# Norm rows and key operands of a feature map lifted in fewer, larger transfers

## What is computed

```python
def feature_map(x, orf):                      # x: 32 wide, orf: 128 x 32
    proj = x @ orf.T / d_k ** 0.25
    norm = jnp.sum(x * x, axis=-1, keepdims=True) / (2.0 * math.sqrt(d_k))
    return (jnp.exp(proj - norm) + EPS) / math.sqrt(m)
q = feature_map(split(x @ Wq.T + bq), orf)
k = feature_map(split(x @ Wk.T + bk), orf)
v = split(x @ Wv.T + bv)
kv, ksum = einsum('nlm,nld->nmd', k, v), sum(k, axis=1)
out = einsum('nlm,nmd->nld', q, concatenate([kv, ksum]))
attn = (out[..., :-1] / out[..., -1:]) @ Wo.T + bo
x = layernorm(x + attn)
x = layernorm(x + x @ (ternary(weight) * scale).T)
```

## Time and profile before

| | |
|---|---|
| Median of three runs | 1310.24 us (1308.63 to 1312.22) |
| The profiled execution | 1310.11 us, span 1308.2 us |
| TensorE, VectorE, ScalarE, GpSimd busy | 98%, 72%, 54%, 39% |
| Operand lifts on SyncE | 384 + 256 of 128 KB, 64 of 256 KB |
| Norm lifts on GpSimd | 512 of 4 KB |
| Period of a middle batch | about 159 us |

### The profile page before, as it was taken

How to read it: one execution, slowest core, us unless ns; L and a number is a source line. 1 busy time by engine, 2 the same in 40 slices (tenths; PEclk the granted TensorE clock), 3 DMA queues, 4 the chain that set the end, 5 groups by cost and what they waited for, 6 DMA issues and landing times.

```text
span 1308.2 us, 25147 instructions
## 1 busy us (share of the span) xinstructions
PE 1279.2 (98%) x8570; PEld 965.2 (74%) x8570; DVE 946.1 (72%) x1791; ACT 701.9 (54%) x1403; POOL 511.1 (39%) x1005
## 2 busy tenths in 40 slices
PE   9999999999999999999999999999999999999886
PEld 8767787777877678776787768876788767886655
DVE  7599765886668775787657786577765787657866
ACT  5556535564355743657336663367544665346634
POOL 1325433345333443325424344334453334433343
PEclk9999999999999999999999999999999999999999
DMA  7557314763145721567215762257602675036611
GB/s 237 146 129 217 94 46 111 177 176 91 57 123 145 207 67 55 131 152 193 61 57 129 182 165 67 61 136 200 161 33 70 154 202 140 33 95 140 165 33 65
DMA packets 94015, 160.37 MB, mean 123 GB/s; under 512 B 31168, under 2 KB 47680, under 8 KB 93376
## 3 DMA queue, kind: packets, MB, share of 16 engines
q1 hardware_dynamic: 67856, 139.78, 41.5%
q10 hardware_dynamic: 9648, 16.85, 3.4%
q0 software_dynamic: 16384, 2.13, 1.2%
HBM read 39.13 MB, written 16.78 MB: 43 GB/s over the span
## 4 chain that ended last, share of the span: by engine, by line
PE 83%; DVE 5%; ACT 3%; SPq 3%; DMA 3%; issue 2%; POOL 1%; ACTq 0%; POOLq 0%; DVEq 0%
PE ps L927 27%; PE ps L964 24%; PE ps L1025 8%; PE ps L950 4%; PE ps L996 4%; PE ps L952 4%; PE ps L951 4%; PE ps L983 4%; PE ps L1051 2%; DMA rows<-in_x_t 1%; SPq L519 1%; ACT features L671 1%; SPq L508 1%; DMA rows<-in_Wk_t 1%; DMA stacks<-norm_rows 1%
## 5 line engine op out<-in xcount | busy, mean ns | idle before, releaser
L671 ACT ACTIVATE features<-ps 128x512 f32<-128x512 f32 x512 | 278.3, 601 | 257.3 <-PE ps L927 197.5
L574 POOL DMA_DIRECT2D stacks<-norm_rows x512 | 251.4, 499 | 397.4 <-DVE norm_rows L852 173.7
L553 POOL TENSOR_SCALAR stats<-stats 128x1 f32<-128x1 f32 x128 | 36.4, 284 | 317.9 <-DVE stats L780 317.9
L927 PE MATMUL ps<-Wo_hi,stacks 128*128 128x512 f32 x448 | 150.5, 402 | 0.0
L645 ACT ACTIVATE values_then_attention<-ps 128x512 f32<-128x512 f32 x64 | 38.2, 597 | 197.3 <-PE ps L952 194.0
L793 DVE TENSOR_TENSOR den<-den,features 128x512 f32<-128x512 f32 x192 | 132.3, 689 | 13.8 <-ACT features L671 0.4
L927 PE MATMUL ps<-orf_key_a,stacks 128*128 128x256 f32 x512 | 131.7, 289 | 1.1 <-DMA stacks<-norm_rows 1.1
L1025 PE MATMUL ps<-features,kv_ksum 128*32 128x512 f32 x1024 | 123.1, 598 | 5.9 <-ACT features L671 4.6
L927 PE MATMUL ps<-orf_key_b,stacks 68*128 68x256 f32 x512 | 128.5, 283 | 0.0
L829 DVE SCALAR_TENSOR_TENSOR unit_lo<-ps,cols,unit_hi 128x512 fp32r<-128x512 f32 x128 | 94.3, 736 | 35.0 <-ACT squares L655 35.0
L927 PEld LDWEIGHTS ps<-orf_key_a,stacks 128*128 128x128 f32 x512 | 97.1, 190 | 26.9 <-issue 23.0
(11 more groups left out here) (136 smaller groups left out, 2726.6 us busy)
## 6 DMA issues: line engine op xcount, KB each, us to landing
stacks<-unit_hi SPq DMA_DIRECT2D x384, 128.0 KB, 2.4
stacks<-unit_lo SPq DMA_DIRECT2D x256, 128.0 KB, 3.2
stacks<-unit_hi SPq DMA_DIRECT2D x64, 256.0 KB, 3.8
rows<-in_x_t SPq DMA_DIRECT2D x56, 256.0 KB, 3.6
out<-rows ACTq DMA_DIRECT2D x56, 256.0 KB, 2.0
stacks<-norm_rows POOLq DMA_DIRECT2D x512, 4.0 KB, 2.7
rows<-in_x SPq DMA_DIRECT2D x32, 256.0 KB, 4.0
features<-in_x SPq DMA_DIRECT2D x32, 256.0 KB, 4.1
```

Source lines behind the costliest of these rows:

```text
L574: pool.dma_start(slot[row:row + 1, c:c + L].rearrange("o (t c) -> o t c", c=DH), NN[DH * h:DH * (h + 1), u % 2, part, :].bitcast(F32)).the ...
L671: nc.scalar.activation(FE[:, n % 8, :, 0:M], ps[:, :].rearrange("p (a m) -> p a m", a=HG), ACT.Exp, scale=C_EXP).then_inc(a_exp.sem, 1)
L927: last = mm(out, a, b, start=(n == 0), stop=(n == len(terms) - 1))
```

## The change

Norm rows: a query unit's four heads go in one transfer per part (source of 128 partitions, one destination row of 16 KB), a key unit's in one transfer per part and pair of heads (source of 64 partitions, two destination rows of 4 KB). Key operands: the high and low part of a pair of heads are now stacked as 64 partitions of high and 64 of low, so that a pair's high part is one lift, also in blocks one and two; `MA` is filled to match. The order of key lifts on SyncE is now blocks one and two high, blocks three and four high, then, after the wait for the low part, blocks one and two low.

```diff
-        KEY_LIFTS, QUERY_LIFTS = 10, 12
+        KEY_LIFTS, QUERY_LIFTS = 6, 12
...
-        n_lifted = [Signal("norms_lifted_even", 2 * HG * NG, 0, 16), Signal("norms_lifted_odd", 2 * HG * NG, 0, 16)]
+        KEY_NORMS, QUERY_NORMS = 4, 2
+        n_lifted = [Signal("norms_lifted_even", NG * KEY_NORMS, 0, 16), Signal("norms_lifted_odd", NG * QUERY_NORMS, 0, 16)]
...
-                eng.wait_ge(sig.sem, sig.nth(b, 2 * HG * (u // 2 + 1)))
+                eng.wait_ge(sig.sem, sig.nth(b, (KEY_NORMS if is_key(u) else QUERY_NORMS) * (u // 2 + 1)))
...
+                    if is_key(u):
+                        pairs = [(p, slice(2 * DH * p, 2 * DH * (p + 1))) for p in range(2)]
+                        for first_col in (0, 2 * L):
+                            for p, rows in pairs:
+                                c = first_col + L * p
+                                sp.dma_start(slot[0:2 * DH, c:c + L], hi[rows, :]).then_inc(sig.sem, 16)
+                        wait(v_plo.sem, v_plo.nth(b, 2 * u + 2))
+                        for p, rows in pairs:
+                            sp.dma_start(slot[2 * DH:4 * DH, L * p:L * (p + 1)], lo[rows, :]).then_inc(sig.sem, 16)
+                        continue
...
-                for h in range(HG):
-                    for part in range(2):
-                        row, c = (2 * DH + 2 * part + h % 2, L * (2 + h // 2)) if is_key(u) else (3 * DH + part, L * h)
-                        pool.dma_start(slot[row:row + 1, c:c + L].rearrange("o (t c) -> o t c", c=DH),
-                                       NN[DH * h:DH * (h + 1), u % 2, part, :].bitcast(F32)).then_inc(n_lifted[u % 2].sem, 16)
+                for part in range(2):
+                    if is_key(u):
+                        for p in range(2):
+                            row, c = 2 * DH + 2 * part, L * (2 + p)
+                            pool.dma_start(slot[row:row + 2, c:c + L].rearrange("o (t c) -> o t c", c=DH),
+                                           NN[2 * DH * p:2 * DH * (p + 1), u % 2, part, :].bitcast(F32))\
+                                .then_inc(n_lifted[0].sem, 16)
+                    else:
+                        row = 3 * DH + part
+                        pool.dma_start(slot[row:row + 1, :].rearrange("o (t c) -> o t c", c=DH),
+                                       NN[:, u % 2, part, :].bitcast(F32)).then_inc(n_lifted[1].sem, 16)
...
                 for r in range(4):
-                    a = r // 2
+                    a = r % 2
                     nc.vector.tensor_copy(MA[DH * r:DH * (r + 1), M * a:M * (a + 1)], wT[DH * r:DH * (r + 1), 0:M])
```

More of the change, by code:

```diff
@@ L503, in _ @@
                         continue
+                    if is_key(u):
[8 more added lines that the diff above has]
+                        continue
                     for h in range(HG):
                         src = hi[DH * h:DH * (h + 1), :]
[L506 to L515, removed]
+                        sp.dma_start(slot[0:DH, L * h:L * (h + 1)], src).then_inc(sig.sem, 16)
+                        sp.dma_start(slot[2 * DH:3 * DH, L * h:L * (h + 1)], src).then_inc(sig.sem, 16)
                     wait(v_plo.sem, v_plo.nth(b, 2 * u + 2))
                     for h in range(HG):
-                        r, c = (2 * DH * (h % 2) + DH, L * (h // 2)) if is_key(u) else (DH, L * h)
-                        sp.dma_start(slot[r:r + DH, c:c + L], lo[DH * h:DH * (h + 1), :]).then_inc(sig.sem, 16)
+                        sp.dma_start(slot[DH:2 * DH, L * h:L * (h + 1)], lo[DH * h:DH * (h + 1), :]).then_inc(sig.sem, 16)
         @block.gpsimd
```

## The result

The changed kernel took 1314.52 us in the median (1312.26 to 1317.19) beside 1311.01 us for the kernel before, eight executions of each: a ratio of 1.0031, 95% interval 1.0019 to 1.0042. The forecast was 1305.2 us, within 1302.5 to 1311.5. So the change costs some 4 us instead of giving 5. The profiled execution took 1315.79 us, with a span of 1314.0, 5.8 us more than the span of the profile before.

What follows compares the result with a forecast made beforehand. TensorE, busy 1279.2 of 1308.2 us, was taken as the bound, so only its waits could be won. Gains of 2.1 + 1.1 + 1.8 = 5.0 us from 1310.2 gave 1305.2 us, range 1302.5 to 1311.5.

Steps and rivals of the forecast that it cites:

- The last unit, 2.1 us: Last unit's query features: TensorE's 2.44 us wait on norm rows falls to 0 to 0.5, winning 2.1 us.
- The key wait, 1.1 us: Batch 2: TensorE's single 1.1 us wait on norm rows before key features goes entirely; bounds 0 and 1.1 us.
- The load of tile 4, 1.8 us gained: End of stage 4: fewer lifts let the next batch's tile 4 load go earlier, ending ScalarE waits of 1.8 us.
- The rival of the few engines: Key norms with two destination partitions use two DMA engines and land late; middle 1330 us, chance 0.14.
- the point of decision: Key norm landing of about 7 us; each microsecond beyond costs up to 24 us over 3 units in 8 batches.
- The price of the drain: On few engines, 32 norm rows alternating with lift pieces need 32 x 143 ns = 4.6 us more to land.
- the three signs: Forecast wrong if key norms land after 7 us, issue exceeds a microsecond, or TensorE's waits fall without the time.
- the 0.5 of the sum: GpSimd's assumed issue cost per norm transfer, 0.5 us whatever its rows; upper bound 1.0 us key, 2.0 us query.

Runs made afterwards that it cites:

- query norms alone: Kernel before with query norms in two transfers, key norms still in eight, ten key lifts: 1308.33 us, ratio 0.9989.
- two forms with the tile moved: Tile 4's load put ahead of the low lifts, in the changed kernel (1307.07 us) and in the kernel before with one-partition key norms and twelve key lifts (1304.28 us).
- the form with paced lifts: Kernel before with six wider key lifts and a small extra transfer behind each high lift, so ten issues again: 1313.78 us, ratio 1.0034.
- the regrouped form: Kernel before with key blocks holding heads p and p + 2, four one-partition key norm transfers, two query ones, twelve key lifts: 1309.34 us, ratio 0.999.
- the form with query norms and the moved tile: Kernel before with query norms in two transfers and tile 4's load ahead of the low lifts: 1306.63 us, ratio 0.996.
- the changed kernel with the moved tile: Changed kernel with the next batch's tile 4 load between high and low lifts of unit 6: 1307.07 us; taken again 1308.07 us, ratio 0.9978.
- the norm part: Kernel before with only the change's norm transfers, four per key unit and two per query unit: 1318.27 us, ratio 1.0062.
- the runs of each part: Kernel before with the change's norm transfers only (1318.27 us, ratio 1.0062), and with its six key lifts only (1317.16 us, ratio 1.0052).

## Why the prediction was wrong

**The last unit, 2.1 us: the wait went as reckoned, the size holds by luck.** Query norms land after a median of 2.7 us and cost GpSimd 0.59 us each; the wait in front of the last query features fell from 2.44 us to 0.43, ended by ScalarE. But 0.84 us are new at the sum matmul, behind VectorE's last addition, so that 1.2 us of waiting are gone. The rest is TensorE's clock, which the prediction didn't look at. In the kernel before it was granted at half for 3.4 us behind the wait of 2.44:

```profile
1241.70:1245.10 3.40, 3.40 (x43) 2.15 (x42) 2.30 (x4) 1.57 (x3) 0.00 (x0) 0.50 0.17 62
```

The three matmuls behind that wait took 1.42 us, and 0.95 in the changed kernel. The stretch from the last key features to the end shows what this is worth. It is 69.2 us in the kernel before, and 67.1 with query norms alone and 67.0 in two forms with the tile moved (1305.2 - 1238.2 and 1303.2 - 1236.2). But it is 67.7 in the form with paced lifts, which still waits 2.58 us there and kept full clock behind that wait. So with the clock at full the shorter wait is worth some 0.7 us, an estimate from one execution of each. And the clock can fall in this stretch without that wait: in the profiled execution of the changed kernel the stretch is 69.2 as before, with half clock from about 1251.2 to 1254.6 us and a granted clock of 0.77 in the last 18 us, where it was 0.95; it is 68.5 in the regrouped form, 68.6 in the form with query norms and the moved tile, and 68.9 in the changed kernel with the moved tile when it was taken again.

**The key wait, 1.1 us: right.** 0.6 us in two places are left.

**The load of tile 4, 1.8 us gained: this step failed,** and with the sign. SyncE did issue it earlier, by 1.9 us in batch 3. In batch 2, for which I took 3.3, it was some 2.9 us against TensorE's own work. The wrong step is "the lifts end in the engines at about 431.8, the tile ... landed perhaps two microseconds later, 434.8". It rests on 250 GB/s from a window in which the engines were 0.85 busy. In the changed kernel the engines are fully busy from 588 to 596:

```profile
588.00:592.00 4.00, 4.00 (x21) 2.80 (x24) 1.82 (x4) 4.00 (x13) 2.69 (x4) 1.00 1.06 211
592.00:596.00 4.00, 3.80 (x24) 1.61 (x16) 3.25 (x7) 2.71 (x6) 0.00 (x0) 1.00 1.03 218
```

At 211 and 218 GB/s the 1.57 MB take 7.2 to 7.4 us and not 6.3, and the queue also held the norm transfers, which I had costed for their own readers only. From its issue to its landing the load took 5.7 to 7.1 us in the seven batches, where the step allows it some 5.5 (429.3 to 434.8). And the lower bound was wrong in kind: I wrote "0, if the load is held by the transfers ahead of it". Nothing excludes that a load issued earlier into a fuller queue lands later than before, and it did, by 1.1 us. The margin was given as less than a microsecond; a price with such a margin wants a bound on the other side of zero.

**The rival of the few engines had the right mechanism and the wrong victim.** I asked whether the norm rows' own readers would wait, found the point of decision at a landing of 7 us, and they land after 5.4 us (median), so that TensorE hardly waits for them. What shares the engines with them waits instead. Alone the norm part costs 0.62%. The price of the drain was misread too. The 128 ns that I took for a lift's 4 KB piece is the mean over all packets of that queue; its 4096 B packets took 291 ns in the median. And 32 norm rows aren't 32 turns beside the lifts' pieces: they go in one packet of 4096 B. The case should have been priced from the row of the load instead of the row of the first reader: that load had 435.54 - 432.77 = 2.8 us to land without anyone waiting, and took 3.0.

**What I priced at nothing** was the pace of the lifts for the norm rows, which alone costs key features 6.6 us in six batches. In the changed kernel the smaller number of norm transfers covers it. So the change holds two losses and one cure, which only the runs of each part showed. None of the three signs that the prediction named as its refutation came (norms landing later than 7 us, where the latest took 6.9; an issue of over a microsecond; TensorE's waits down without the time). The waits themselves rose, which these signs didn't cover.

**The rest:** a key transfer's issue on GpSimd costs 0.68 us with two partitions and 0.53 with one, both near the 0.5 of the sum and far from the 1 to 2 us of its upper bound. GpSimd's pauses in front of norm transfers came to 13.4 us before and 3.2 after. A stall of 2.09 us also cost TensorE its clock in batch 3, which no term had: the 16 matmuls and the eight behind them took 4.64 us by the chain, and 3.08 in the kernel before.

## To carry to other kernels

When a queue is cut into fewer and larger transfers, look for the load that stands right behind them and for who waits for it: its landing counts, not its issue. A transfer that must be there soon goes ahead of bulk that has time (in the changed kernel one load moved was worth 0.49%, in the kernel before it doesn't show). In on-chip transfers of short rows from GpSimd, try one destination partition; two partitions were slower than one for the same rows. And where a term is a wait of TensorE, read the granted clock behind it in both kernels: a part of the 2.1 us here was clock.

## What the hardware showed that I had not expected

A norm transfer of 64 rows of 128 B into two partitions took two packets of 4096 B and 0.68 us of GpSimd, and into one partition 16 packets of 512 B and 0.53 us; the queue's mean packet was 72 and 31 ns. TensorE's clock was at half for some 3.4 us behind an idle stretch of 2.09 us in the changed kernel and of 2.44 in the kernel before. But it stayed at full speed behind 2.19, 2.42 and 2.11 us in the kernel with the norm part alone and behind 2.58 in that with paced lifts. A stall of 2.69 us in the norm part alone was again followed by half speed (0.50 in the window from 122 to 124 us). Length of the stall alone doesn't tell the two apart here; what does is left open.
